# Second layer of a four-layer kernel: the preparation of a batch begins 24 of 64 positions sooner, and the second norm gets its own buffer

## The reference, cut to what matters

```python
xa = _ln(x, ln1_w, ln1_b)
sx = concat([state - xa[:, :1], xa[:, :-1] - xa[:, 1:]])
xxx = tanh((xa + sx * maa_x) @ maa_w1)           # five mixes
xm = xa + sx * (maa_stack + xxx @ maa_w2)        # -> xk, xw, xv, xr, xg
w = exp(-exp(time_decay + tanh(xw @ td_w1) @ td_w2))
r, k, v, g = xr @ Wr.T, xk @ Wk.T, xv @ Wv.T, silu(xg @ Wg.T)
def step(s, rkvw):
    a = k_t[..., :, None] * v_t[..., None, :]
    out = einsum('bhi,bhij->bhj', r_t, u * a + s)
    s = a + w_t[..., :, None] * s
og = groupnorm(out) * gn_w + gn_b
x1 = x + og * g @ Wo.T
xc = _ln(x1, ln2_w, ln2_b)                       # the second norm
rr = sigmoid((xc + sx2 * ffn_maa_r) @ Wfr.T)     # the channel mix
kk = square(relu((xc + sx2 * ffn_maa_k) @ Wfk.T))
return x1 + rr * (kk @ Wfv.T)
```

## Time and profile before

| | us |
|---|---|
| median of 3 runs | 5401.21 (5399.8 to 5409.04) |
| the profiled execution | 5402.98 |
| its span in the profile | 5401.3 |
| second layer in the span: from PE's first mean of batch 0 to its last product of batch 7 | 962.8 to 2240.3 |
| one full iteration of the loop (b = 3) | 146.7 |

### The profile page before, as it was taken

One profiled execution on the slowest core, in us unless ns is written; L12 is line 12 of the kernel. 1 busy time (PEld: TensorE's weight loads), 2 busy tenths in 40 slices (PEclk: granted clock), 3 DMA queues, 4 the chain that ended last, 5 costly groups with the idle time before them and its releaser, 6 DMA issues. The chain is left out here.

```text
span 5401.3 us, 77906 instructions
## 1 busy us (share of the span) xinstructions
PE 4526.6 (84%) x22864; PEld 3322.8 (62%) x22864; DVE 3106.7 (58%) x6291; ACT 2059.6 (38%) x3977; POOL 1674.3 (31%) x1127
## 2 busy tenths in 40 slices
PE   6999998578888887488888797987888977988886
PEld 3444443456666555377676586875676855877764
DVE  5555553276666667276673474754675744757642
ACT  2444444223333331254452353542444532544421
POOL 1223222244444444122223223223223233232240
PEclk8998898779888888799998898998899988999999
DMA  0000000200000000111112212112111122121123
GB/s 33 20 25 16 20 20 5 94 9 13 11 2 12 12 9 8 52 52 58 49 52 77 70 55 60 48 59 85 57 48 56 56 65 80 59 60 44 55 70 106
DMA packets 123227, 240.96 MB, mean 45 GB/s; under 512 B 16884, under 2 KB 34036, under 8 KB 121824
## 3 DMA queue, kind: packets, MB, share of 16 engines
q1 hardware_dynamic: 119520, 225.31, 13.2%
q0 software_dynamic: 3456, 12.58, 0.6%
HBM read 220.79 MB, written 16.78 MB: 44 GB/s over the span
## 5 line engine op out<-in xcount | busy, mean ns | idle before, releaser
L1733 POOL TENSOR_TENSOR c_wl<-c_wr,c_wh 128x512 fp32r<-128x512 f32 (+1 forms) x576 | 827.6, 1441 | 1926.4 <-ACT c_wh L1961 1682.3
L1779 PE MATMUL c_ps<-c_hh,c_wh 128*128 128x512 f32 x768 | 321.9, 419 | 144.9 <-POOL c_hl L1739 144.9
L2012 ACT ACTIVATE c_pr<-c_ps,c_nms 128x257 f32<-128x257 f32 x512 | 244.0, 477 | 483.7 <-DVE c_nms L2166 481.4
L1378 POOL TENSOR_TENSOR b_sb<-b_sb,b_rt 128x1024 f32<-128x1024 f32 x128 | 283.0, 2211 | 362.7 <-DVE b_sb L1418 362.7
L572 ACT ACTIVATE a_ex<-a_ps 128x1024 f32<-128x1024 f32 x256 | 261.2, 1023 | 346.3 <-PE a_ps L408 346.0
L1779 PE MATMUL c_ps<-c_wh,c_cth 128*128 128x256 f32 x1024 | 300.5, 293 | 98.7 <-POOL c_wl L1733 98.5
L666 DVE TENSOR_REDUCE a_nm<-a_ps 128x2 f32<-128x1024 f32 x256 | 310.7, 1218 | 76.1 <-PE a_ps L385 73.2
L1418 DVE TENSOR_TENSOR_SCAN b_sb<-b_wt,b_s,b_ps 128x256 f32<-128x256 f32 x512 | 348.5, 726 | 5.4 <-issue 3.0
L1961 ACT ACTIVATE c_wh<-c_wr 128x512 fp32r<-128x512 f32 (+1 forms) x448 | 302.2, 683 | 67.7 <-DMA c_wr<-in_wv 50.8
L1779 PE MATMUL c_ps<-c_gh,c_wh 128*128 128x512 f32 x768 | 311.5, 406 | 13.0 <-ACT c_g L2061 10.0
L1780 PE MATMUL c_ps<-c_hl,c_wh 128*128 128x512 f32 x768 | 319.7, 416 | 0.0
(11 more groups left out here) (313 smaller groups left out, 11255.2 us busy)
## 6 DMA issues: line engine op xcount, KB each, us to landing
c_wr<-in_downs SPq DMA_DIRECT2D x192, 256.0 KB, 2.7
c_wr<-in_wv SPq DMA_DIRECT2D x64, 512.0 KB, 4.3
c_wr<-in_wq SPq DMA_DIRECT2D x128, 256.0 KB, 2.8
c_wr<-in_wk SPq DMA_DIRECT2D x128, 256.0 KB, 3.4
c_wr<-in_fc SPq DMA_DIRECT2D x64, 256.0 KB, 2.9
b_w<-in_w SPq DMA_DIRECT2D x8, 1024.0 KB, 13.2
a_x<-in_x SPq DMA_DIRECT2D x8, 512.0 KB, 3.9
a_ctx<-in_ctx SPq DMA_DIRECT2D x8, 512.0 KB, 4.3
```

The lines of the kernel that those rows point to most:

```text
L1378: pool.tensor_tensor(SB[:, quad % 3, :, 0:L], SB[:, quad % 3, :, 0:L], RT[:, scan % 2, q // 4, :].unsqueeze(1).broadcast_to([P, 4, L]), AL ...
L1733: pool.tensor_tensor(piece(WL, slot), piece(WR, slot), piece(WH, slot), ALU.subtract).then_inc(piece_cut[slot], 1)
L1779: pe.matmul(out, sh, mh, start=start, stop=False, skip_group_check=True)
L2012: act.activation(PR[:, i, 0:L + 1], ps[:, BS + 1 - i % 2, 0:L + 1], ACT.Exp, bias=NMS[:, i:i + 1], scale=float(K2) ** -0.5, accum_out=RS[: ...
```

## The change

The preparation of a batch is rotated against the other two phases by `LEAD = 24` positions. In iteration b of 1 and more, position n of the loop issues position n + 24 of the preparation of batch b + 1 as long as that is under 64, and after that (n from 40 on) position n + 24 - 64 of the preparation of batch b + 2. Iteration -1 holds the whole preparation of batch 0, as before. Iteration 0 holds the 88 positions that bring the rotation about (all 64 of batch 1, the first 24 of batch 2), 1 or 2 of them at each n. Iteration 6 has positions 24 to 63 of batch 7 only. V moves from 47, 49 to 49, 52, G from 55, 57 to 59, 61, and the gate on DVE from G + 7 = 62 to G + 4 = 63. The second norm works in `ZB` instead of `OG`, and POOL's wait for `p_xp` goes.

```diff
-        AT_K, AT_R, AT_TW1, AT_TW2, AT_BONUS, AT_V, AT_G = 27, 33, 38, 40, 43, 47, 55
+        AT_K, AT_R, AT_TW1, AT_TW2, AT_BONUS, AT_V, AT_G = 27, 33, 38, 40, 43, 49, 59
...
+        LEAD = 24
+
+        def preparation(b, n):
+
+            if b < 0:
+                items = [(0, n)]
+            elif b == 0:
+                items = [(1 + i // STEPS, i % STEPS) for i in range(n * (STEPS + LEAD) // STEPS, (n + 1) * (STEPS + LEAD) // STEPS)]
+            else:
+                i = n + LEAD
+                items = [(b + 1 + i // STEPS, i % STEPS)]
+            return [(t, m) for t, m in items if t < B]
...
-                    act.activation(SQB[:, :, :], OG[:, s % 2], ACT.Square).then_inc(p_sq, 1)
+                    act.activation(SQB[:, :, :], ZB[:, :, :], ACT.Square).then_inc(p_sq, 1)
...
-                    if t >= 2 and i == 0:
-                        pool.wait_ge(p_xp, t - 1 + AHEAD)
...
-                    pool.tensor_tensor(OG[:, s % 2], OG[:, s % 2], SDB[:, :].unsqueeze(1).broadcast_to([P, EC, L]), ALU.mult).then_inc(p_xn, 1)
+                    pool.tensor_tensor(ZB[:, :, :], ZB[:, :, :], SDB[:, :].unsqueeze(1).broadcast_to([P, EC, L]), ALU.mult).then_inc(p_xn, 1)
...
-                if n == AT_G + 7:
+                if n == AT_G + 4:
                     dve.wait_ge(pa_read, t * UNITS + U_G + 2 + AHEAD)
...
-                    if pre is not None:
-                        pre_stage(pre, n)
+                    for t, m in preparation(b, n):
+                        pre_stage(t, m)
```

More of the change, by code:

```diff
@@ L903, in stages @@
         def stages(b):
-            return (b if 0 <= b < B else None), (b + 1 if b + 1 < B else None), (b - 1 if b >= 1 else None)
+            return (b if 0 <= b < B else None), (b - 1 if b >= 1 else None)
+        LEAD = 24
[8 more added lines that the diff above has]
+            return [(t, m) for t, m in items if t < B]
         def at(n, first, count, every=1):
@@ L1029, in pre_stage @@
                     mm.then_inc(mix_ps, 1)
-                for first, unit, e, w in ((AT_K, U_K, 0, W_K), (AT_R, U_R, 1, W_R), (AT_V, U_V, 3, W_V), (AT_G, U_G, 4, W_G)):
-                    i = at(n, first, 2, 2)
+                for first, every, unit, e, w in ((AT_K, 2, U_K, 0, W_K), (AT_R, 2, U_R, 1, W_R), (AT_V, 3, U_V, 3, W_V), (AT_G, 2, U_G, 4, W_G)):
+                    i = at(n, first, 2, every)
                     if i is not None:
@@ L1141, in _ @@
             for b in range(-1, B + 1):
-                scan, pre, post = stages(b)
+                scan, post = stages(b)
                 for n in range(STEPS):
@@ L1217, in pre_stage @@
                     act.activation(BON[:, 2 * i:2 * i + 2, :], both(PA), ACT.Copy).then_inc(pa_read, 1)
-                i = at(n, AT_V, 2, 2)
+                i = at(n, AT_V, 2, 3)
                 if i is not None:
@@ L1273, in post_stage @@
                     for k in range(EC):
-                        act.activation(XPB[:, k, 1:L + 1], OG[:, s % 2, k, :], ACT.Identity, scale=VEC[:, V_LN2W, k:k + 1], bias=VEC[:, V_LN2B, k:k + 1])
+                        act.activation(XPB[:, k, 1:L + 1], ZB[:, k, :], ACT.Identity, scale=VEC[:, V_LN2W, k:k + 1], bias=VEC[:, V_LN2B, k:k + 1])
                     act.drain().then_inc(p_xp, 1)
@@ L1447, in pre_stage @@
                     dve.tensor_tensor(XF[:, e % 2], XF[:, e % 2], SXA[:, :, :], ALU.mult).then_inc(xm_ready, 1)
-                i = at(n, AT_V + 3, 2, 2)
+                i = at(n, AT_V + 3, 2, 3)
                 if i is not None:
@@ L1479, in post_stage @@
                     dve.wait_ge(gated, s + 1 + AHEAD)
-                    dve.tensor_tensor(OG[:, s % 2], XB[:, :, :], half(PB, 0).unsqueeze(1).broadcast_to([P, EC, L]), ALU.subtract).then_inc(p_xc, 1)
+                    dve.tensor_tensor(ZB[:, :, :], XB[:, :, :], half(PB, 0).unsqueeze(1).broadcast_to([P, EC, L]), ALU.subtract).then_inc(p_xc, 1)
                 if n == AT_VAR + 2:
```

2 lines of the change are left out of this document (1 added, 1 removed).

## The result

The changed kernel takes 5418.61 us (median of 12 runs) against 5400.51 for the kernel before (12 runs); the ratio is 1.0031, 95% interval 1.0021 to 1.0041. It is slower, by 18 us, where 57 us less were forecast. The profiled execution took 5408.33 us with a span of 5406.7. It reached the second layer at 953.4 us instead of 962.8, in code that is the same, so the layer is compared from scan to scan: from the first scan of batch 0 to the end of the last of batch 7 it takes 1103.7 us against 1086.5, 17.2 more.

A forecast was written before the change was run, and what follows sets the result against it. PE was taken as nearest to a bound, busy 126.1 of 146.7 us per full iteration. Iteration 0 + 8, iteration 1 - 8, iterations 2 to 5 - 39, iteration 6 - 18: together - 57, so 5344 us; range 5275 to 5398.

The forecast's parts named there:

- The first four gaps: PE's idle gaps in a full iteration: 3 us before K, 2.4 at n = 32, 1.3 before G's second unit, 6 to 7 at 44.
- six table loads per iteration: ScalarE (ACT): square roots alternating with tanh or exp need six table loads instead of four, 1.28 us each, mostly while waiting for PE.
- no cost of the buffer: Second norm in ZB, free from Wo's last unit (24) to FK's input (42): costs nothing, adds no instruction.
- The loads per quarter: PE's work by quarters of 16 positions in a full iteration, counted as 31.8, 28.7, 25.7, 25.7 us after the change.
- the first norm's (45 to 55) [is covered] by FR: Full iteration, n = 45 to 55: FR's work on PE was to cover the first norm's chain; no wait priced there.
- The forecast of 137: Full iteration: 137 us instead of 146.7, from a walk of 131 with 19 idle plus 7 for the clock.
- one drop of the clock, behind the gap at 44: About 17 us at half rate meeting FK behind PE's gap of 6 to 7 us, costing 7 us per full iteration.
- Iteration 0: Start of the loop, 24 positions more: + 8 us (4 to 12), of which 7.0 for the norm.
- Iteration 6: End of the loop, 24 positions less: 129 us instead of 146.7, entered in the sum as - 18.
- iteration 1: First iteration after the start: 144.0 to 136 us, - 8.
- the clock takes it back: Rival, 0.15: new gaps in three quarters drop PE's clock to a mean of 0.77; iteration 152 us, + 39, so 5440.
- No net effect: Rival, 0.07: POOL slows more of DVE's mix multiplies and inputs, 10 us per iteration, cancelling the gain; 5400 us.

The follow-up runs named there:

- experiment 1: Changed kernel with only the rotation taken back (LEAD = 0), moved V, G, gate and ZB kept: 5405.26 us, ratio 1.0006 to the kernel before.
- Experiment 2: Changed kernel with the first norm's variance at position 4 instead of 5, so its square root precedes ACT's read of FK's second unit: 5382.09 us, ratio 0.9966.
- experiment 4: Changed kernel with 13 unused matmuls added on PE ahead of the spread at n = 44 in iterations 1 to 5: 5388.81 us, ratio 0.9973.
- experiment 6: Changed kernel with variance at 4 and the 13 added matmuls ahead of the spread at n = 44 together: 5379.40 us, ratio 0.9966.
- 10: Changed kernel with LEAD = 0 and 9 unused matmuls ahead of the spread at n = 4 in iterations 1 to 5: 5418.32 us, ratio 1.0032.
- 12: Changed kernel with 7 unused matmuls ahead of the spread at n = 52 in iterations 1 to 5: 5419.88 us, ratio 1.0035.
- 3: Changed kernel with the 24 extra preparation positions in iteration -1 instead of iteration 0: 5415.05 us, ratio 1.0025.
- 8: Changed kernel with the 24 extra positions spread over iterations 0 to 3, six each: 5416.91 us, ratio 1.0031.
- Experiment 14: Changed kernel with variance at 4 and batch 1's gate issued on DVE just ahead of batch 2's first subtraction: 5376.69 us, ratio 0.9955.
- 5: Changed kernel with G two positions earlier (57, 59), the gate still at 63: 5412.55 us, ratio 1.0022.
- 11: Changed kernel with variance at 4 and the 24 extra positions in iteration -1: 5377.70 us, ratio 0.9957.
- 13: Changed kernel with variance at 4 and, in iteration 0, batch 1's positions at n = 0 to 39, batch 2's at 40 to 63: 5383.27 us, ratio 0.9968.
- 7: Changed kernel with variance at 4 and G two positions earlier together: 5395.18 us, ratio 0.9988.

## Why the prediction was wrong

**What held.** The first four gaps with their places and, but for that at G, their sizes; six table loads per iteration; no cost of the buffer (experiment 1); no stall for loads; PE's work for 24 positions, forecast as 9.3 us less in iteration 6 and measured as 10.4 more in iteration 0 (from 70.4 to 80.7, busy time weighted by quarters). The loads per quarter held only roughly. The work in the quarters cut by DVE's scans is 27.3, 33.0, 26.9 and 21.8 us, forecast 31.8, 28.7, 25.7 and 25.7; before it was 14.6, 28.2, 24.9 and 42.9, where the same count by positions had given 13.1, 31.5, 36.3 and 31.1. The count did not match the kernel that was known, and the text did not say so.

**The step that failed in the full iteration** is "the first norm's (45 to 55) [is covered] by FR". It looked at PE's work only. The root stands at n = 46 on ACT, behind the read of a product that PE makes last, and FR's first read at 51 stands behind the scaling at 50. I had followed what lies on PE and DVE beside the chain, and not what stands ahead of it on ACT: DVE stood 8.12 us and PE 3.40 + 2.25 us. Experiment 2 moved one number and gave 7.1 us per iteration, to 139.9, of which 2.6 are idle time. The forecast of 137 is nearly that kernel's, in part by luck: its idle time was right (19 against 19.9), but it had 112 us of work where there are 109, and 7 us of half rate where there are 10.8. For the four iterations 2 to 5 this term was - 39 and is about 0.

**The second term mis-sized is half rate.** I gave 7 us for one drop of the clock, behind the gap at 44, and nothing for the rest; measured are 15.5 in all, and 2.3 right behind that gap. The price of 7 was read from one stretch of 17 us at half rate in the kernel before; here the stretch was 6.7 us, with PE idle for 2.2 of them. The others stand at the small gaps, and the costliest, 5.1 us, where PE is busy with short products. That small gaps could cost was to be seen in the earlier trace rows, 0.62 behind gaps of 1.2 us. But the length of a gap does not decide it either. In the kernel before, PE also stood for 1.38 us in its last quarter, and the clock stayed at 1.00:

```profile
1584.40 3.72 PE L990 MATMUL b_ps<-b_xf,b_w 128*128 128x256 f32 x16 [1.38 <-ACTq L1227]
```

Nor do the losses have each its own price: 2 and 4 do not add (experiment 6), and filling gaps in other places gave nothing (10, 12).

**Iteration 0**, forecast + 8 and measured + 27.3, was sized as seven us of norm and one for the rest; more than 12 was named as a sign of being wrong. Its idle time on PE rose by 15.8 us, from 25.4 to 41.2 (139.8 - 98.6), its work by 10.4 and its half rate by 1.1; these are the 27. The 8 us hold the norm beside the scans and about 1 us for the added work, though the prediction had counted 9.3 us of it in iteration 6. Experiments 3 and 8 show that the price goes with the positions: 27 to 29 us in iteration -1, in iteration 0, or over four. Experiment 14 shows one mechanism, DVE in order before the gate, at 3.7 us. The rest is not split; that 88 positions at 64 n leave fewer scans between the steps of every chain is argued from DVE's waits for the mixes (19.5 us against 9.5 before), not shown.

**Iteration 6** gave 13.8 of the 17.7 forecast, **iteration 1** + 3.2 instead of - 8, for the same reason as the full ones.

Of the rivals, "the clock takes it back" is nearest in the full iterations: it named 36 us of idle and half rate together as the point from which nothing is won, and 38.0 were measured. Its price of + 39 was wrong, as the mean clock stayed at 0.87. "No net effect" (5400) came nearest in time and was wrong in mechanism: of the 40 mix multiplies in the changed kernel (L1458) none took over 1.23 us, where the longest was 2.79 before, and as many channel-mix inputs as before, 7 of 64, took over 1 us. No rival had what decided the sign: + 27.3 at the start against - 13.8 at the end, with nothing in between.

On the table load the trace decides against the figure from the Trainium skill ("ScalarE: Activation LUTs", What ACT_TABLE_LOAD costs): the root starts 1.29 us after its load does (1602.43 to 1603.72 in the changed kernel), and the instruction ahead of the load ended 0.02 us before it, so no further 1.4 us are seen here. It is so in three of the six loads of an iteration; in the others ACT waits between the load and its user.

## What to carry to other kernels

When work is shifted between phases in engines that run in order, follow each chain through the queue of every engine it touches, the lightly loaded one too: what stands one position ahead of each step, and when that is released. This rotation paid 27 us at its start and got 14 back at its end, so the repeated part has to gain more than the difference; price the start from a run in which the same steps stand bare. An idle gap ahead of heavy TensorE work can have two prices, the gap and half rate, and only a run tells the second. Nor does the gain of an edit say what its own place was worth: look at the clock in the whole iteration, as much of the half rate that experiments 2 and 4 won back lay elsewhere.

## What the runs showed of the hardware that was not expected

Thirteen matmuls with no use, put where PE stood for 6.9 us, made the kernel 30 us faster than without them (experiment 4). In two other places the same gave nothing (10, 12). Half rate right behind the gap was 2.3 us an iteration; the rest of the gain was in other places.

The clock also fell where PE was busy. Timeline of PE in the changed kernel around the stretch from 1528.5 to 1538.8, in which PE is busy for 10.27 of 10.30 us at a granted clock of 0.50:

```profile
1528.21 1.83 PE L1065 MATMUL b_ps<-b_tw 64*128 64x256 f32 x4 [1.01 <-ACTq L1224]
1529.97 1.08 PE L991 MATMUL b_ps<-b_sb,b_selg 128*32 128x256 f32 x8
1531.08 2.05 PE L1075 MATMUL b_ps<-b_za,b_bo 128*128 128x256 f32 x4
```

What ran were short products, most of few rows or few columns, behind a single gap of 1.01 us. Whether their shape or the gap did it was not tested. In the kernel before, the clock was 0.57 from 1523 to 1527, with PE busy throughout and no gap over 0.44 us in the 10 us ahead, so a gap of 1 us is not needed for it.

Full iterations in quite different orders came out at the same length: before, the change, and experiments 3, 5, 10 and 12 all at 146.5 to 147.1 us; 2, 11, 13 and 14 at 139.9 or 140.0; 4, 6 and 7 at two lengths in turn. Why was not tested.
